# Column attention in an eight-stage transformer kernel: plain query and key projections, their split parts placed by DMA instead of computed in place

## The chip, the cores and the metric

The kernel runs on one core of one Trainium2 chip. The metric is the device time of one execution in microseconds. TensorE (PE) does matmuls, VectorE (DVE), ScalarE (ACT) and GpSimd (POOL) the elementwise work; SyncE (SP) only issues DMA transfers, in the order in which its program lists them.

## The reference, cut to what matters

The model is six residual stages with layer norms. The change touches only the last one, the attention in `_L1_ffn_ref`, which attends along the columns of a 16 x 256 x 128 tensor after a reshape:

```
ln1 = _ln(hidden_states, ln1_weight, ln1_bias)
qkv = (ln1 @ qkv_weight.T).reshape(S, B, N_KV, (Q_PER_KV + 2) * HEAD_DIM)
q = qkv[..., :q_dim]; k, v = ...               # 16 query heads, 8 key/value heads of 8
scores = einsum('sbhd,tbhd->bhst', q, k) / sqrt(8)
attn = softmax(where(causal, scores, -1e9))
```

A head has only 8 dimensions, so a score matmul contracts over very few rows. The scores are wanted to near float32, while the fast matmul type (fp32r) rounds its operands. So the kernel writes q = q_hi + q_lo and k = k_hi + k_lo and contracts over 24 rows that hold the products q_hi k_hi + q_hi k_lo + q_lo k_hi.

## The kernel before, in words

The stage is `column_attention` (line 2379 on). It works on 8 groups of 512 tokens (`U = 8`, index u), and each group has 8 pairs of heads (`PAIRS`), so 64 pair steps g. In pair step g, PE makes the straight scores of pair g (two mask matmuls `bar`, L2569, and 8 score matmuls, L2575), DVE takes their row maxima (L2905), and PE makes the transposed scores of pair g - 11 (L2584, `LAG = 11`), which now include the maxima as two more rows; ACT exponentiates them (L2767). Every second step PE multiplies four heads' probabilities with the values (`values`, L2597).

PE may begin the masks of pair g + 1 only when DVE has finished the maxima of pair g (`negmax_ready`): a chain from PE to DVE to PE runs through every step. Everything else is hung on the steps by the list `stages` (offset, name): a stage with offset o runs for group u in step 8u + o, after the step's scores, and each engine's program is that order, fixed. So step 8u + r repeats for every group, and I call it step r of a group below. `PlannedRing` deals out four PSUM banks by planned hold times; a stage that opens a bank waits until the bank's last reader is done.

Around the change:

- `wq`, `wk` (`cq_pad`, `ck_pad`) are padded weights: for every group of four heads, 4 x 32 columns, in which the 8 columns of a head stand three times. They are copied out of a transposed PSUM tile by nine small activations at the start (L2707, L2709).
- `project` (L2554) is one matmul of 128x128 by 128x512 in float32 for each of the six pieces q0, k0, q1, k1, q2, q3, in steps 5, 6, 7 of the group before and 0, 1, 3 of the own one (offsets -3, -2, -1, 0, 1, 3).
- `round_qk` (ACT, L2731 and L2733) rounds a piece to fp32r; the key's pad rows get ones. `split_qk` (DVE, L2834) computes rounded * split + PSUM, where `split` is 0 or -1 or so by row, and so makes hi or lo rows; it writes straight into `qT` or `kT`, [128, 4 or 2, 512], which the score matmuls read. It also frees the bank.
- `place_rows` (SP, L3001): four transfers of 16 KB put the row maxima into two rows of every head in `qT`.
- `hold_clock` (L232) issues dummy matmuls in steps 0 to 10, while there are no transposed scores yet, and in the drain.

Of the kernel before, what the change touches and what calls it, by code (L numbers as in the profile page):

```python
# [2393 lines left out]
def column_attention(nc, A, K, x_in, R, acc_all, hn_rows):  # L2394
# [6 lines left out]
    with ExitStack() as ctx:  # L2401
# [10 lines left out]
        def sets(n, name, shape, dt=F32):  # L2412
# [8 lines left out]
        split, pad_ones = K["split"], K["pad_ones"]  # L2421

        wq = sb("cq_pad", [P, GROUPS, 4, 32])
        wk = sb("ck_pad", [P, KG, 4, 32])
# [29 lines left out]
        rounded = sets(2, "c_rounded", [P, W], F32R)  # L2454
        qT = sets(2, "cqT", [P, GROUPS, W], F32R)
# [25 lines left out]
        v_cleared = sem("c_values_cleared")  # L2481
        masks_ready = sem("c_masks_ready")
# [7 lines left out]
        rounded_ready = Counted(sem("c_rounded_ready"))  # L2490
        scores_full = Counted(sem("c_scores_full"))
# [29 lines left out]
            (-3, "q0"), (-2, "k0"), (-1, "q1"), (0, "k1"), (1, "q2"), (3, "q3"),  # L2521
# [6 lines left out]
        projections = [("q", 0), ("k", 0), ("q", 1), ("k", 1), ("q", 2), ("q", 3)]  # L2528

        def turn_of(u, name, g):  # L2530
            return len(projections) * u + projections.index((name, g))
# [4 lines left out]
        def _(pe):  # L2536
# [13 lines left out]
            def project(u, name, w, g):  # L2550
                if name == "q" and g == 0:
                    ring.wait_read(pe, "lnT", u)
                ps = ring.open(pe, name, u, g, held=0.95)
                pe.matmul(ps[:], w[:, g].rearrange("p j d -> p (j d)"), lnT[u][:], start=True, stop=True)\  # L2554
                    .then_inc(ring.filled(name, u, g), 1)

            def v_(u):
                if u == 0:
                    pe.wait_ge(w_ready, 1)
# [12 lines left out]
            def scores(n, i, t):  # L2572
                u, p = divmod(n, PAIRS)
                g, j = p // 2, 32 * (2 * (p % 2) + i)
                mm = pe.matmul(s_ps[:, i, t, :], qT[u][j:j + 3 * DH3, g, t * P:(t + 1) * P],  # L2575
                               kT[u][j:j + 3 * DH3, g % KG, t * P:(t + 1) * P], start=False, stop=True, skip_group_check=True)
                if t == TG - 1:
                    mm.then_inc(scores_full.sem, 1)

            def scores_T(n, i, t):  # L2580
                u, p = divmod(n, PAIRS)
                g, j = p // 2, 32 * (2 * (p % 2) + i)
                rows_read = 3 * DH3 + 2
                mm = pe.matmul(t_ps[:, i, t, :], kT[u][j:j + rows_read, g % KG, t * P:(t + 1) * P],  # L2584
                               qT[u][j:j + rows_read, g, t * P:(t + 1) * P], start=False, stop=True, skip_group_check=True)
# [16 lines left out]
            def pair_step(g):  # L2602
# [21 lines left out]
                if turned:  # L2624
                    n = g - LAG
                    if n % PAIRS == 0:
                        pe.wait_ge(*rows_placed.at(64 * (n // PAIRS + 1)))
# [63 lines left out]
            for g in range(KG):  # L2691
                steps[f"k{g}"] = lambda u, g=g: project(u, "k", wk, g)
            for g in range(GROUPS):
                steps[f"q{g}"] = lambda u, g=g: project(u, "q", wq, g)
# [6 lines left out]
        def _(act):  # L2701
            act.wait_ge(cleared, 2)
# [664 lines left out]
```

## Time and profile before

| | us |
|---|---|
| median of 3 runs | 1921.08 (1919.87 to 1923.79) |
| the profiled execution | 1923.63 |
| its span | 1921.9 |
| mean granted TensorE clock, share of full | 0.947 |

Over the whole span PE is busy 89%, DVE 72%, ACT 62% and POOL 54%. The column attention lies from about 1409 to 1659 us of the span. Its first straight scores start at 1425.3 us, those of step 11 at 1452.7, and the last at about 1607; then the last eleven pairs' transposed scores, the output projections and the router drain until 1659. Before and after it stand stages that the change does not touch; each ends with a meeting of all engines. In a row of a timeline the columns are start, duration, engine, line, operation, output and inputs, count, and in brackets the engine's idle time before it and what ended it. A matmul's own duration contains its fill and drain; what it costs its engine is the distance to the next start.

### The profile page before, as it was taken

What the parts mean: (1) busy time and instruction counts of PE and PEld (TensorE: products, weight loads), DVE (VectorE), ACT (ScalarE), POOL (GpSimd) and SP (SyncE); (2) the same over time, 40 slices, a digit from 0 to 9 for tenths busy, and PEclk for the clock granted to TensorE, in tenths of its full rate; (3) what the DMA queues carried; (4) which work ended last, traced back from release to release, by engine and by line L of the source; (5) the groups of instructions that cost most, each with busy time, mean ns of one, the idle gap of its engine ahead of it and who ended that gap; (6) DMA issues with size and microseconds to landing.
All of it is one profiled execution on the core that took longest, in us unless ns stands there. A gap on an engine that the chain in (4) does not pass through costs nothing. (4 is left out here: it accounts for less than half of the span.)

```text
span 1921.9 us, 43928 instructions
## 1 busy us (share of the span) xinstructions
PE 1709.4 (89%) x15676; PEld 1307.0 (68%) x15676; DVE 1376.4 (72%) x4609; ACT 1189.0 (62%) x2858; POOL 1037.9 (54%) x1590
## 2 busy tenths in 40 slices
PE   7999999989889999999999999999879999589930
PEld 4666666656777777777777777776656667479930
DVE  6788888872767788888888888988657876611127
ACT  3566666643688877778878777776315776244412
POOL 3466676663255665656666566666422432175375
PEclk9999999998899999999999999999888999689975
DMA  3000000000300000000000000000000000345322
GB/s 60 6 13 16 16 16 16 12 5 10 92 1 2 1 2 7 8 7 8 7 9 7 8 2 6 5 5 9 6 24 15 27 21 16 99 70 76 59 65 84
DMA packets 57824, 44.03 MB, mean 23 GB/s; under 512 B 13952, under 2 KB 50186, under 8 KB 57482
## 3 DMA queue, kind: packets, MB, share of 16 engines
q1 hardware_dynamic: 52330, 30.11, 5.5%
q0 software_dynamic: 4608, 9.45, 3.4%
q8 instruction: 129, 2.11, 0.5%
q10 hardware_dynamic: 672, 1.67, 0.2%
q14 instruction: 85, 0.70, 0.1%
HBM read 26.52 MB, written 13.63 MB: 21 GB/s over the span
## 5 line engine op out<-in xcount | busy, mean ns | idle before, releaser
L2288 POOL TENSOR_SCALAR probs<-probs,rsums 128x128 f32<-128x128 f32 (+1 forms) x512 | 208.6, 426 | 294.8 <-DVE rsums L2185 293.9
L1061 POOL TENSOR_SCALAR at_least<-magnitudes,candidates 128x512 bf16<-128x512 f32 x128 | 198.2, 1564 | 149.2 <-DVE candidates L950 149.2
L1906 ACT ACTIVATE probs<-probs,low 128x130 f32<-128x130 f32 (+1 forms) x512 | 227.7, 460 | 6.3 <-DVE low L2169 6.2
L2169 DVE CUSTOM_DVE_ANT_0 probs<-dist,pq,nmin 128x128 f32<-128x128 f32 (+1 forms) x512 | 181.2, 409 | 67.6 <-PE pq L1622 67.5
L1021 DVE TENSOR_REDUCE negmax<-ps_scores 128x4 f32<-128x1024 f32 x128 | 156.2, 1221 | 51.3 <-PE ps_scores L629 49.6
L812 ACT ACTIVATE pT<-ps_scoresT 128x1024 f32<-128x1024 f32 x128 | 131.1, 1024 | 63.6 <-PE ps_scoresT L638 57.3
L2179 DVE COPY pT<-pq 128x384 f32<-128x384 f32 x256 | 129.8, 547 | 3.8 <-PE pq L1637 3.8
L1817 ACT ACTIVATE qn<-pq 128x512 f32<-128x512 f32 x128 | 77.2, 603 | 72.2 <-PE pq L1479 70.5
L1622 PE MATMUL pq<-k1T,q1T 64*128 64x128 f32 (+1 forms) x1024 | 119.3, 351 | 0.5 <-ACT k1T L1832 0.4
L3309 POOL DMA_INDIRECT m_x<-token_rows,m_idx_put x80 | 75.7, 947 | 80.2 <-DVE m_idx_put L3239 33.3
L3261 DVE COPY m_y<-pm 128x256 f32<-128x256 f32 x40 | 17.0, 424 | 140.0 <-PE pm L3147 140.0
L1906 ACT ACTIVATION_READ_ACCUMULATOR probs<-probs,low 128x1 f32 x512 | 104.3, 204 | 0.0
L2094 DVE TENSOR_REDUCE ss<-sq 128x8 f32<-128x512 f32 x128 | 84.2, 675 | 26.0 <-ACT sq L1820 25.1
L2905 DVE TENSOR_REDUCE cnegmax<-pc_scores 128x8 f32<-128x1024 f32 x64 | 78.2, 1222 | 25.6 <-PE pc_scores L2575 25.5
L1637 PE MATMUL pq<-ident,probs 128*128 128x128 f32 x512 | 91.3, 274 | 0.0
L2942 POOL TENSOR_SCALAR crstd<-cmv 128x4 f32<-128x4 f32 x16 | 3.7, 233 | 159.6 <-DVE cmv L2816 159.6
L2767 ACT ACTIVATE cpT<-pc_scoresT 128x1024 f32<-128x1024 f32 x64 | 65.5, 1024 | 33.6 <-PE pc_scoresT L2584 33.4
L1622 PEld LDWEIGHTS pq<-k1T,q1T 64*128 64x128 f32 x1024 | 67.5, 187 | 23.2 <-issue 22.2
L1657 PE MATMUL pr_heads<-pT,v 128*64 128x256 f32 x512 | 83.2, 404 | 0.1
L1671 PE MATMUL pr_out<-wo,o1T 128*128 128x128 f32 x512 | 78.5, 276 | 3.5 <-DVE l_r L2026 3.5
L1634 PE MATMUL pq<-ident,probs 128*128 128x128 f32 x256 | 77.3, 302 | 3.7 <-POOL probs L2288 3.6
L3147 PEld LDWEIGHTS pm<-m_w,m_hid 128*128 128x128 f32 x640 | 77.6, 192 | 2.0
(546 smaller groups left out, 5296.1 us busy)
## 6 DMA issues: line engine op xcount, KB each, us to landing
expert_answers<-m_y SPq DMA_DIRECT2D x40, 128.0 KB, 2.1
m_w<-in_L_ffn_moe_w_dram SPq DMA_DIRECT2D x16, 256.0 KB, 5.9
x<-in_x_dram SPq DMA_DIRECT2D x16, 128.0 KB, 2.2
x_mid<-x SPq DMA_DIRECT2D x16, 128.0 KB, 1.8
y<-x_mid SPq DMA_DIRECT2D x16, 128.0 KB, 2.3
x_mid<-y SPq DMA_DIRECT2D x16, 128.0 KB, 1.8
cx<-x_mid SPq DMA_DIRECT2D x8, 256.0 KB, 2.9
token_rows<-c_hn SPq DMA_DIRECT2D x8, 256.0 KB, 2.0
```

Of the source, the lines that this page charges most:

```text
L812: act.activation(pT[:, n % NPT].rearrange("p i k n -> p (i k n)"), t_ps[:].rearrange("p i k n -> p (i k n)"), ACT.Exp).then_inc(pT_ready.s ...
L1021: dve.tensor_reduce(negmax[u][:, :, j:j + 2, q].rearrange("p t j -> p j t"), s_ps[:], AX.X, ALU.max, negate=True).then_inc(negmax_ready.se ...
L1061: pool.tensor_scalar(at_least[:, a, :], mags[:, 512 * (a // 2):512 * (a // 2) + 512], cf[:, a:a + 1], None, ALU.is_ge).then_inc(mask_ready ...
L1622: mm = pe.matmul(ps[i][:, t * P:t * P + w], q1T[u][64 * i:64 * i + 64, p, t * P:(t + 1) * P], k1T[u][64 * i:64 * i + 64, p, 0:w], start=Tr ...
L1637: mm = pe.transpose(ps[:, (kt + 1) * P:(kt + 2) * P], probs[:, a + 1, first_key + kt * P:first_key + (kt + 1) * P], ident[:])
L1657: pe.matmul(tgt[:, 0:N], v1[u][:, 0, h * DH1:(h + 1) * DH1], pT[:, b, 0:2].rearrange("k t q -> k (t q)"), start=True, stop=False, skip_gro ...
L1671: mm = pe.matmul(y_ps[:, u % 2, t * D:(t + 1) * D], o1T[:, n % 4, t * P:(t + 1) * P], wo1[:, p, :], start=(p == 0 and t == 0), stop=False, ...
L1906: ins = act.activation(probs[:, a, keys_nulls(i, w)], probs[:, a, keys_nulls(i, w)], ACT.Exp, bias=low[:, a, i:i + 1], scale=-1.0, accum_o ...
L2094: dve.tensor_reduce(ss[:, a, t, 8 * j:8 * j + 8], sq[:, j, :].rearrange("p (h d) -> p h d", d=DH1), AX.X, ALU.add).then_inc(ss_ready.sem, 1)
L2169: ins = dve.tensor_tensor_reduce(probs[:, a + t, keys(i, w)], dist[:, (1 - t) * P:N], ps[:, t * P:t * P + w], slopes[h], nmin[u][:, t, h:h ...
L2179: dve.tensor_copy(pT[:, (2 * m + i) % 4].rearrange("k t q -> k (t q)"), ps[:, 0:3 * P])\
L2288: ins = pool.tensor_scalar(probs[:, a + t, keys(i, w)], probs[:, a + t, keys(i, w)], rsums[:, a + t, i:i + 1], 1.0, ALU.mult, ALU.mult)
```

## The change

All six padded projections are replaced by two plain ones, q (128 columns, all 16 heads) in step 2 of the group before and k (64 used columns) in step 3 of it. ACT rounds each once, DVE makes the rest (PSUM minus rounded) once, into `q_parts` and `k_parts`. Seven transfers on SP's queue then place the parts into the heads' rows: hi, hi, lo and a row of zeros for q (256 KB of destination each), hi, lo, hi for k (128 KB each). A head now takes 32 rows, in which dimension d has rows 4d to 4d + 3; the key's fourth rows are ones, set once at the start, and the two row maxima go into two of the query's fourth rows. The scores contract over 32 rows instead of 24 and 26. `qT` gets a third buffer. The first scores of group u wait for the seven transfers.

```diff
-        wq = sb("cq_pad", [P, GROUPS, 4, 32])
-        wk = sb("ck_pad", [P, KG, 4, 32])
+        wq = sb("cq_turned", [P, 4, DH3, GROUPS])
+        wk = sb("ck_turned", [P, 2, 4, DH3, KG])
...
-        rounded = sets(2, "c_rounded", [P, W], F32R)
-        qT = sets(2, "cqT", [P, GROUPS, W], F32R)
+        q_parts = sets(2, "cq_parts", [P, 2, W], F32R)
+        k_parts = sets(2, "ck_parts", [64, 2, W], F32R)
+        no_rows = sb("c_no_max_rows", [P, W])
+        qT = sets(3, "cqT", [P, GROUPS, W], F32R)
...
-            (-3, "q0"), (-2, "k0"), (-1, "q1"), (0, "k1"), (1, "q2"), (3, "q3"),
+            (-6, "q"), (-5, "k"),
...
-            (-3, "split_q0"), (-2, "split_k0"), (-1, "split_q1"), (0, "split_k1"), (1, "split_q2"), (3, "split_q3"),
+            (-6, "rest_q"), (-5, "rest_k"), (-5, "place_qk"),
...
-                mm = pe.matmul(s_ps[:, i, t, :], qT[u][j:j + 3 * DH3, g, t * P:(t + 1) * P],
-                               kT[u][j:j + 3 * DH3, g % KG, t * P:(t + 1) * P], start=False, stop=True, skip_group_check=True)
+                mm = pe.matmul(s_ps[:, i, t, :], qT[u][j:j + 32, g, t * P:(t + 1) * P],
+                               kT[u][j:j + 32, g % KG, t * P:(t + 1) * P], start=False, stop=True, skip_group_check=True)
...
-                    if p % 2 == 0:
-                        ring.wait_read(pe, "q", u, p // 2)
-                        if p // 2 < KG:
-                            ring.wait_read(pe, "k", u, p // 2)
+                    if p == 0:
+                        pe.wait_ge(*qk_placed[u % 2].at(PLACED * (u // 2 + 1)))
...
-            for n in range(3):
-                for i in range(2):
-                    act.activation(wq[:, KG * i:KG * i + KG, :, n * DH3:(n + 1) * DH3], w_ps[:, :, :, i * DH3:(i + 1) * DH3],
-                                   ACT.Copy, scale=1 / math.sqrt(DH3))
-                act.activation(wk[:, :, :, n * DH3:(n + 1) * DH3], w_ps[:, :, :, 2 * DH3:3 * DH3], ACT.Copy)
+            for i in range(2):
+                act.activation(wq[:, :, :, KG * i:KG * i + KG].rearrange("k a d g -> k g a d"),
+                               w_ps[:, :, :, i * DH3:(i + 1) * DH3], ACT.Copy, scale=1 / math.sqrt(DH3))
+            act.activation(wk[:, 0].rearrange("k a d g -> k g a d"), w_ps[:, :, :, 2 * DH3:3 * DH3], ACT.Copy)
...
+            def round_qk(u, name, parts, p):
+                ps = ring.wait(act, name, u)
+                if u >= 2 and name == "q":
+                    act.wait_ge(*qk_placed[u % 2].at(PLACED * (u // 2)))
+                act.activation(parts[u][:, 0, :], ps[0:p, :], ACT.Copy).then_inc(rounded_ready.sem, 1)
...
+            def rest_qk(u, name, parts, p):
+                ps = ring.bank(name, u)
+                dve.wait_ge(*rounded_ready.at(2 * u + (1 if name == "q" else 2)))
+                dve.tensor_tensor(parts[u][:, 1, :], ps[0:p, :], parts[u][:, 0, :].bitcast(F32), ALU.subtract)\
+                    .then_inc(ring.read(name, u), 1)
...
+            pool.memset(no_rows[:], 0.0)
+            for i in range(3):
+                ins = pool.memset(kT[i][:].bitcast(F32), 1.0)
+            ins.then_inc(keys_set, 1)
...
-                    for j in range(4):
-                        sy.dma_start(qT[u][32 * j + 3 * DH3:32 * j + 3 * DH3 + 2].bitcast(F32),
-                                     rowsT[u][8 * j:8 * j + 8].bitcast(F32)).then_inc(rows_placed.sem, 16)
+                    sy.dma_start(qT[u][3:P:16].bitcast(F32), rowsT[u][:].bitcast(F32)).then_inc(rows_placed.sem, 16)
+
+                def place_qk(u):
+                    placed = qk_placed[u % 2].sem
+                    if u == 0:
+                        sy.wait_ge(keys_set, 1)
+                    if u >= 3:
+                        sy.wait_ge(*pT_ready.at(PAIRS * (u - 2)))
+                    ring.wait_read(sy, "q", u)
+                    for part, half in enumerate((0, 0, 1)):
+                        sy.dma_start(qT[u][part:P:4].bitcast(F32), q_parts[u][:, half, :].bitcast(F32)).then_inc(placed, 16)
+                    sy.dma_start(qT[u][3:P:4].bitcast(F32), no_rows[:]).then_inc(placed, 16)
+                    ring.wait_read(sy, "k", u)
+                    for part, half in enumerate((0, 1, 0)):
+                        sy.dma_start(kT[u][part:P:4].bitcast(F32), k_parts[u][:, half, :].bitcast(F32)).then_inc(placed, 16)
```

## Rows read from the trace of the kernel before

**Rows 1.** Busy time by engine in stretches: length, PE, PEld, DVE, ACT, POOL, PEclk, DMA.
```profile
1425.30:1452.70 27.40, 24.83 (x188) 15.77 (x188) 21.38 (x30) 7.24 (x12) 9.37 (x16) 0.94 0.02 6
1518.10:1591.30 73.20, 68.12 (x1070) 50.23 (x1068) 58.12 (x118) 51.59 (x73) 25.70 (x33) 1.00 0.07 23
1591.30:1610.10 18.80, 16.56 (x312) 12.58 (x311) 14.56 (x29) 12.23 (x18) 5.64 (x7) 1.00 0.06 21
```

**Rows 2.** Timeline of PE through one steady group, step 1 to step 0.
```profile
1518.12 0.39 PE L2569 MATMUL pc_scores<-c_barred,c_one_hot 24*128 24x512 bf16 x2
...
1519.69 1.13 PE L2554 MATMUL pc<-clnT,cq_pad 128*128 128x512 f32 x2 [0.78 <-DVE ckT L2834]
...
1522.48 0.39 PE L2569 MATMUL pc_scores<-c_barred,c_one_hot 24*128 24x512 bf16 x2
...
1524.61 0.39 PE L2569 MATMUL pc_scores<-c_barred,c_one_hot 24*128 24x512 bf16 x2 [0.70 <-DVE cnegmax L2905]
...
1529.71 0.39 PE L2569 MATMUL pc_scores<-c_barred,c_one_hot 24*128 24x512 bf16 x2
...
1532.94 0.39 PE L2569 MATMUL pc_scores<-c_barred,c_one_hot 24*128 24x512 bf16 x2
...
1536.38 0.39 PE L2569 MATMUL pc_scores<-c_barred,c_one_hot 24*128 24x512 bf16 x2
...
1540.07 0.39 PE L2569 MATMUL pc_scores<-c_barred,c_one_hot 24*128 24x512 bf16 x2
...
1542.52 0.39 PE L2569 MATMUL pc_scores<-c_barred,c_one_hot 24*128 24x512 bf16 x2
```

**Rows 3.** Timeline of PE, last group, where no projections of a next group are left.
```profile
1602.17 0.39 PE L2569 MATMUL pc_scores<-c_barred,c_one_hot 24*128 24x512 bf16 x2 [0.73 <-DVE cnegmax L2905]
...
1604.49 0.39 PE L2569 MATMUL pc_scores<-c_barred,c_one_hot 24*128 24x512 bf16 x2
...
1607.14 0.39 PE L2569 MATMUL pc_scores<-c_barred,c_one_hot 24*128 24x512 bf16 x2
...
1609.96 0.43 PE L2649 MATMUL pc<-c_ident_r,c_rows 128*32 128x128 f32 x4
```

**Rows 4.** Groups of instructions by shape within that steady group: busy, mean ns, idle before.
```profile
L2905 DVE TENSOR_REDUCE cnegmax<-pc_scores 128x8 f32<-128x1024 f32 x8 | 9.8, 1220 | 3.3 <-PE pc_scores L2575 3.3
...
L2584 PE MATMUL pc_scoresT<-cqT,ckT 26*128 26x128 f32 x64 | 6.0, 304 | 0.0
L2575 PE MATMUL pc_scores<-ckT,cqT 24*128 24x128 f32 x64 | 5.9, 301 | 0.0
...
L2834 DVE SCALAR_TENSOR_TENSOR cqT<-c_rounded,split_rows,pc 128x512 fp32r<-128x512 f32 x4 | 3.0, 748 | 0.7 <-ACT c_rounded L2731 0.2
```

**Rows 5.** Timeline of all engines at the start of the stage.
```profile
1409.30 2.73 POOL L2924 MEMSET cv<- 128x1024 f32 x3
...
1416.16 1.11 DVE L2826 TENSOR_SCALAR cxn<-cx,cmv,crstd 128x128 f32<-128x128 f32 x4 [1.53 <-POOLq L2951]
...
1423.05 0.71 DVE L2834 SCALAR_TENSOR_TENSOR cqT<-c_rounded,split_rows,pc 128x512 fp32r<-128x512 f32 x1
...
1425.32 0.39 PE L2569 MATMUL pc_scores<-c_barred,c_one_hot 24*128 24x512 bf16 x2 [1.70 <-issue]
```

**Rows 6.** Timeline of SP's queue in a steady group.
```profile
1518.83 2.59 SPq L3001 DMA_DIRECT2D cqT<-c_rowsT  x4
1521.46 0.39 SPq L2989 DMA_DIRECT2D cx<-x_mid  x1
```

**Rows 7.** DMA issues of the stage (KB, landing), packets and share in 1545.8:1549.5.
```profile
cx<-x_mid SPq DMA_DIRECT2D x8, 256.0 KB, 2.9
...
q1 hardware_dynamic: 164, 0.29, 26.9%
```

**Rows 8.** PE at step 11, and the stretch behind it (columns as in Rows 1).
```profile
1452.69 0.39 PE L2569 MATMUL pc_scores<-c_barred,c_one_hot 24*128 24x512 bf16 x2 [1.35 <-DVE cnegmax L2905]
...
1454.00:1458.00 4.00, 4.00 (x28) 2.30 (x26) 2.42 (x3) 2.18 (x3) 0.00 (x0) 0.50 0.01 4
```

More of the change, by code:

```diff
@@ L2490, in column_attention @@
         rounded_ready = Counted(sem("c_rounded_ready"))
+        qk_placed = [Counted(sem(f"c_qk{i}_placed")) for i in range(2)]
         scores_full = Counted(sem("c_scores_full"))
@@ L2548, in ln_T, with project, v_ @@
                 mm.then_inc(ring.filled("lnT", u), 1)
[L2550 to L2557, printed above, removed]
+            def project(u, name, w):
                 if u == 0:
                     pe.wait_ge(w_ready, 1)
+                ring.wait_read(pe, "lnT", u)
+                ps = ring.open(pe, name, u, held=0.95)
+                pe.matmul(ps[:], w, lnT[u][:], start=True, stop=True).then_inc(ring.filled(name, u), 1)
+            def v_(u):
                 ring.wait_read(pe, "lnT", u)
@@ L2582, in scores_T @@
                 g, j = p // 2, 32 * (2 * (p % 2) + i)
[L2583 to L2585 removed]
+                mm = pe.matmul(t_ps[:, i, t, :], kT[u][j:j + 32, g % KG, t * P:(t + 1) * P],
+                               qT[u][j:j + 32, g, t * P:(t + 1) * P], start=False, stop=True, skip_group_check=True)
                 if t == TG - 1:
@@ L2690, in _ @@
             steps = dict(lnT=ln_T, v=v_, turn_rows=lambda u: u < U - 1 and max_rows(u), back=back, project_out=project_out, hT=h_T, logits=router)
-            for g in range(KG):
-                steps[f"k{g}"] = lambda u, g=g: project(u, "k", wk, g)
+            steps["q"] = lambda u: project(u, "q", wq[:].rearrange("p j d g -> p (j d g)"))
+            steps["k"] = lambda u: project(u, "k", wk[:].rearrange("p a j d g -> p (a j d g)"))
             for g in range(GROUPS):
-                steps[f"q{g}"] = lambda u, g=g: project(u, "q", wq, g)
                 steps[f"heads_T{g}"] = lambda u, g=g: heads_T(GROUPS * u + g)
@@ L2722, in norm1 @@
                 affine(lnT[u][:], ps[:], ln1).then_inc(ring.read("lnT", u), 1)
-            def round_qk(u, name, g):
-                n = turn_of(u, name, g)
-                ps = ring.wait(act, name, u, g)
-                if n >= 2:
-                    before = projections[(n - 2) % len(projections)]
-                    ring.wait_read(act, before[0], (n - 2) // len(projections), before[1])
-                if name == "q":
-                    act.activation(rounded[n][:], ps[:], ACT.Copy).then_inc(rounded_ready.sem, 1)
-                else:
-                    act.activation(rounded[n][:], ps[:], ACT.Identity, bias=pad_ones[:]).then_inc(rounded_ready.sem, 1)
+            def round_qk(u, name, parts, p):
[3 more added lines that the diff above has]
+                act.activation(parts[u][:, 0, :], ps[0:p, :], ACT.Copy).then_inc(rounded_ready.sem, 1)
             def read_v(u):
@@ L2776, in _ @@
             steps = dict(lnT=norm1, v=read_v, turn_rows=lambda u: u < U - 1 and max_rows(u), back=back, hT=h_T, logits=router)
-            for name, g in projections:
-                steps[f"{name}{g}"] = lambda u, name=name, g=g: round_qk(u, name, g)
+            steps["q"] = lambda u: round_qk(u, "q", q_parts, P)
+            steps["k"] = lambda u: round_qk(u, "k", k_parts, 64)
             with act.Fori(0, NG // U) as it:
@@ L2909, in _ @@
                          residual0=lambda u: residual(u, 0), residual1=lambda u: residual(u, 1), pick=pick, masks=masks)
-            for name, g in projections:
-                steps[f"split_{name}{g}"] = lambda u, name=name, g=g: split_qk(u, name, g)
+            steps["rest_q"] = lambda u: rest_qk(u, "q", q_parts, P)
+            steps["rest_k"] = lambda u: rest_qk(u, "k", k_parts, 64)
             for g in range(GROUPS):
@@ L3009, in store_rows @@
                     sy.dma_start(token_rows[u], hn[u][:]).then_inc(hn_stored[u % 2], 16)
-                run_in_order(stages, PAIRS, U, dict(load=load, turn_rows=place_rows, hT=store_rows), pair_step)
+                run_in_order(stages, PAIRS, U, dict(load=load, turn_rows=place_rows, place_qk=place_qk, hT=store_rows), pair_step)
                 for i in range(2):
```

20 lines of the change are left out of this document (5 added, 15 removed).

## The prediction

> **What bounds the kernel now.** I read three views in this order. First the busy time by stretches: in the steady stretch 1518.1 to 1591.3 (three groups of 24.4 us) PE is busy 68.1 of 73.2 us at full granted clock, DVE 58.1, ACT 51.6, and the DMA engines are nearly idle at 0.07 [rows 1]. So PE is the engine that could be the bound, at 93%, and DVE is next at 79%. Then PE's timeline through one group, because a share says nothing of which wait ends last in a step. The starts of the mask matmuls give the step lengths [rows 2]: step 1 takes 4.36 us, step 2 2.13, steps 3 and 4 5.10 together, step 5 3.23, step 6 3.44, step 7 3.69, step 0 2.45; in sum 24.40. Two kinds of step stand side by side. In most PE simply has that much to do. Step 2 ends with PE idle for 0.70 us behind DVE's maxima: this is the chain scores, maxima, next masks, and it gives the least length of a step, 2.13 us. Step 1 holds a third thing, PE idle for 0.78 us before q2, because its bank still waits for DVE's split of k1 [rows 2].
>
> The third view is the same kernel's own experiment. In the last group there is no next group to project for, so its steps 5, 6 and 7 lack q0, k0 and q1. They take 2.32 and 2.65 us, and step 7 2.82 up to the row matmuls that follow it [rows 3], against 3.23, 3.44 and 3.69. So taking a projection off a step is worth 0.91, 0.79 and 0.87 us there. The removed matmuls are on the path.
>
> **Part 1: a steady group.** Step by step, with 0.85 us for a projection (the mean of those three) and 0.75 for a DVE pass over 128x512 [rows 4]:
> - Steps 5, 6, 7 lose a projection each: -2.56 us, read off directly.
> - Step 1 loses q2 and the wait before it. That leaves 4.36 - 0.85 - 0.78 = 2.73; a part of the rest is also behind DVE, and I take -1.7.
> - Step 0 loses k1 but already stands at 2.45, and 2.13 is the least; DVE has the first residual behind the maxima. I take -0.25.
> - Step 3 loses q3 and gains k: 0.
> - Step 2 gains q (0.85), of which 0.70 fills PE's idle time: +0.2. DVE there has maxima 1.22 [rows 4], half a residual with its moments, about 1.3, and the new rest of q 0.75, 3.3 us in one step: it starts the next maxima late. I take +0.25 more in steps 3 and 4.
>
> Sum: -2.56 - 1.7 - 0.25 + 0.45 = -4.06 us a group, 24.4 to 20.3. Bounds: had no step a limit but PE, four projections at 0.91 and the 0.78 would give -4.4; if DVE's 3.3 us step delays everything behind it in full (by 1.2 us, 3.3 less 2.13), -3.1.
>
> The other removed work buys nothing of its own: four ACT roundings and four DVE splits (4 x 0.75 = 3.0 us of DVE's 19.8 a group) lie beside PE. They matter as cover: DVE falls to 17 of 20.3 us, 84%, so it does not take over on average, only in step 2. The score matmuls go from 24 and 26 rows to 32. Rows of 24 cost 301 ns and of 26 304 [rows 4], so I take zero for six to eight more; the bound is that slope of 1.5 ns a row carried on, 128 matmuls x 10 ns, overlapped in pairs: +0.6 us a group, below which nothing speaks for a gain.
>
> **Part 2: how often.** From step 17 to step 57 there are five groups; three are the steady ones (3 x 4.06 = 12.2), and the two before them have not yet all of the back end, so I take 3.9 each: 7.8. In the last group only q2 and q3 go: 2.0 of its 18.8 us [rows 1] (steps 1 and 3, where k has no next group). Steps 11 to 16: a projection each out of five steps, k into one; 3.2. Steps 0 to 10 take 27.4 us, 2.49 each [rows 1]; without projections the chain allows 2.13, with two or three longer ones 24.5 in all, but I take only 2.0 off for the clock (below). Sum: 12.2 + 7.8 + 2.0 + 3.2 + 2.0 = 27.2 us won.
>
> **Part 3: the start.** Here the added path is bare. POOL gets memsets of 3 x 128x1024 and 128x512 before its old three, which took 2.73 us for the same sizes [rows 5]: +3.2 us. POOL stood at the first roots shortly before 1416, so these, and all behind them, come 0.8 us later (DVE already waits 1.53 us for POOL's sequencer there [rows 5]). Now ACT's copies of the weights shrink from nine to three, but ACT was ready before the first norm. PE's q comes in front of v; DVE's rest of q queues behind the mask constants, as the first split does at 1423.05 [rows 5], so rest of q ends about 1424 and rest of k 0.7 later. Then the seven transfers, which the first scores wait for. SP issues one in 0.39 (the load cx) to 0.65 us (each of the four row transfers) [rows 6]: 2.7 to 4.5 us for seven. The data: 704 packets of 2 KB. In the stretch of a load, 164 packets took 26.9% of 16 engines for 3.7 us, 97 ns each [rows 7], so 704 take 4.3 us over 16 engines, mostly beside the issuing. A 256 KB load lands 2.9 us after its issue [rows 7]. From the end of rest of q, T = 3.5 + 2.9 = 6.4 us (4.9 to 8.5). First scores at 1424 + 6.4 = 1430.4 instead of 1425.3: +5.1 (3.6 to 7.2). PE is idle for those microseconds and may begin at a lower clock; of a 2.13 us step 1.22 is DVE's, so 0.9 is PE's, and doubling that once adds 0.9: 6.0.
>
> The Trainium skill, "DMA: Bandwidth & Descriptors", section on the anatomy of one DMA, gives a transfer about 2.0 us plus its bytes at 436 GB/s; by it the 1.44 MB of a group would be an estimated 5.3 us if all were issued at once, so T would be about a microsecond less than mine. No row here shows an SBUF to SBUF transfer of that size, and the sum above does not use it.
>
> **Part 4: the transfers in the steady state.** Rest of q is done about 4 us after the start of step 2, and the scores that need it start with the next group's step 0, 15.5 us after the start of step 2 at the new pace. That leaves 11.4 us for T = 6.4: hidden, with 5 us to spare. SP has nothing else in that time: the load sits in step 2 before it, the rows in step 0 behind it, and the store in step 5 waits only as long as the 4 us of issuing. The wait that `place_qk` adds, for the last exponentials of three groups ago, falls in step 2 and ends before rest of q. The single row transfer is one issue instead of 2.59 us of four, with three steps to land; cost and gain zero. The waits for a bank: with the new order the values of step 1 take the bank of the rows, not that of the heads, so the 0.2 us wait there goes as well.
>
> **The sum.** 27.2 - 6.0 = 21.2 us off the profiled 1923.63, 1902.4. That execution lies 2.55 us above the median of 1921.08, so against the median 1899.9. I predict 1900. The forecast's own range: 3.1 to 4.4 us a group, which scales 27.2 to 21 and 29, less a start of 3.6 to 8, so gains of 13 to 25: 1896 to 1908.
>
> **The rivals.**
> A. The placing takes the place of the projections (slower). In this trace small transfers of one queue run into each other, but no transfer of 256 KB stands directly behind another between SBUF tiles. If they were worked off one after the other at their full landing time, 2.9 for q and about 2.0 for k's halves, T = 4 x 2.9 + 3 x 2.0 = 17.6. Then the first scores come at 1424 + 17.6, a cost of 16.3 + 0.9, and seven groups are late by 17.6 - 11.4 = 6.2 each, 43: net +33, 1954. It decides from where the start, T - 0.4, and the lateness, 7 (T - 11.4), eat up 27.2: T = 13.4 us. Against it: the queue's share is 0.07, and the packets' own time is 4.3 us.
> B. The clock. After PE idled 1.35 us before step 11, the granted clock of the next stretch was 0.50, the lower level of 1.2 GHz, and PE, without a gap, got 28 matmul records done in 4 us [rows 8], where the steady rate (1070 in 73.2 us [rows 1]) is 58. In steps 0 to 10 the projections that go were filling PE; it would now idle 0.8 us in nearly every step. If those eleven steps and the next six run at the lower level, PE's 0.9 us part of the chain grows by half of itself where only straight scores stand and doubles where both do, 0.4 and 0.9 us a step: 10 us of the 21, 1910. The Trainium skill, "TensorE: Matmul & The Clock Gate", section on oscillation, warns of just this: idle gaps between bursts bring the half rate back; the trace agrees at step 11. Against it: the steady step 2 has 0.70 us of idle time at full clock [rows 1, 2], and the dummy matmuls stay.
> C. DVE's step 2 and ACT's exponentials set the pace: only 2.5 us a group, 17 instead of 27 won, 1910.
> D. A and B in part, T near 13: no change, 1921.
>
> **How the numbers follow.** Forecast 0.57, B 0.12, C 0.12, A 0.11, D 0.08. The range takes the forecast, B and C with their bounds: 1892 to 1914. A change of 0.2%, 3.8 us, is about what a measurement of this kernel tells from none. Faster: forecast, B and C, 0.81; same 0.07; slower 0.12 (A and a little of D).
>
> **What would show it.** Group length, from one step 1 to the next: 20.3 us (right), above 21.5 (C), above 26 with PE waiting on a DMA in step 0 (A). Step lengths of 2.3, 2.65 and 2.8 in steps 5, 6, 7, and about 2.7 in step 1. First scores 5 us later after the stage's start, last of the seven transfers landed 6 to 7 us after rest of q. Eleven first steps in about 25 us, granted clock near 1.00 there; near 0.5 shows B. The forecast is wrong if the steady group is not shorter by at least 3 us, or if the first scores come more than 9 us later.

## The result, and the profile after

| | before | after |
|---|---|---|
| median, same chip | 1921.08 us (1915.56 to 1923.79) | 1908.3 us (1902.56 to 1910.37) |
| ratio, 95% interval | | 0.993 [0.9907, 0.9953] |
| profiled execution, span | 1923.63, 1921.9 | 1910.19, 1908.4 |

The changed kernel is faster by 0.7%, 12.8 us of medians. The forecast was 1900 with a range of 1892 to 1914: sign and range hold, the size is 8 us off, and just outside the forecast's own 1896 to 1908. The measured time lies nearer to rival B's 1910 than to the forecast's 1900, and it was for B and C that the range went up to 1914.

The difference of the two profiled executions is 13.4 us, but only a part belongs to the change. The stages ahead of column attention, which the change does not touch, took 1409.0 us before and 1403.2 after. I therefore measure the stage by itself, from its first GpSimd instruction to the first load of the next stage: 250.0 us before, 242.0 after, and 239.2 when the changed kernel was profiled once more (there the stages ahead took 1409.0). So the stage is 8.0 to 10.8 us shorter in the profiled executions, less than the 12.8 of the medians. The profiled executions of the changed kernel are themselves long ones, 1.9 and 8.3 us above the medians of their kernels; a typical one may have a shorter fill than the 50 us read below, which no run here shows. Starts of the mask matmuls, one pair a step, cut the stage into parts (us):

| part | before | after | difference | predicted |
|---|---|---|---|---|
| stage's start to first scores | 16.30 | 21.38 | +5.1 | +5.1 |
| steps 0 to 16 | 43.58 | 50.01 | +6.4 | -4.3 |
| step 16 | 2.77 | 2.64 | -0.1 | |
| steps 17 to 57, five groups | 119.66 | 100.29 | -19.4 | -20.0 |
| steps 57 to 63 | 15.81 | 14.45 | -1.4 | -2.0 |
| step 63 to the end | 51.84 | 53.19 | +1.35 | |

(The 4.3 are the prediction's 2.0 + 3.2 won, less 0.9 for the clock.) Almost the whole miss is in one line: the fill of the pipeline got longer where it should have got shorter. The drain's 1.35 us belongs to that execution; in the second profile of the same kernel it was 51.76. The five groups, too, took less there, 98.73 us: in the first profile the clock was low once more in their first group, whose first step took 3.87 us instead of 2.32. So the groups are worth 19.4 to 20.9 us against 20.0 predicted.

The page of the changed kernel, busy time with its share of the span, and the granted clock in 40 slices:
```profile
span 1908.4 us, 43715 instructions
...
PE 1692.8 (89%) x15612; PEld 1301.9 (68%) x15612; DVE 1353.6 (71%) x4576; ACT 1168.0 (61%) x2820; POOL 1041.1 (55%) x1594
...
PEclk9999999999999999999999999999975999689975
```
Slices 30 and 31 hold the stage's start and fill: digits 7 and 5. That is where most of the missing microseconds are. The next view is busy time in stretches, columns as in [rows 1], the start first, then the fill, the steady state, and the last group:
```profile
1403.20:1424.60 21.40, 10.72 (x37) 6.69 (x38) 10.07 (x43) 3.28 (x10) 10.87 (x19) 0.64 0.38 110
1424.60:1474.60 50.00, 47.20 (x354) 31.81 (x355) 25.85 (x39) 11.28 (x16) 7.98 (x15) 0.54 0.22 67
...
1517.50:1577.50 60.00, 57.39 (x1044) 45.35 (x1044) 49.02 (x108) 43.35 (x61) 25.74 (x34) 1.00 0.32 100
1577.50:1597.00 19.50, 16.61 (x328) 13.67 (x329) 14.17 (x32) 12.24 (x17) 5.64 (x7) 1.00 0.05 18
```
In the steady state PE is busy 57.4 of 60 us at full clock, 96%, DVE 82% and ACT 72%: PE is still the bound, with less slack than before [rows 1]. The fill shows a trap in reading busy shares. PE is "busy" 94% of it, at a granted clock of 0.54, with 354 matmuls in 50 us, where the steady state has 1044 in 60. The same stretch of the kernel before, steps 0 to 16, with more matmuls in less time at 0.84:
```profile
1425.30:1468.90 43.60, 41.03 (x370) 26.13 (x371) 31.25 (x48) 15.70 (x23) 11.22 (x19) 0.84 0.03 9
```

PE's timeline through one steady group after, which answers to [rows 2]:
```profile
1537.56 0.39 PE L2566 MATMUL pc_scores<-c_barred,c_one_hot 24*128 24x512 bf16 x2 [0.45 <-DVE cnegmax L2890]
...
1539.94 0.39 PE L2566 MATMUL pc_scores<-c_barred,c_one_hot 24*128 24x512 bf16 x2
1540.66 1.12 PE L2554 MATMUL pc<-clnT,cq_turned 128*128 128x512 f32 x2
...
1542.16 0.39 PE L2566 MATMUL pc_scores<-c_barred,c_one_hot 24*128 24x512 bf16 x2
1542.90 1.12 PE L2554 MATMUL pc<-clnT,ck_turned 128*128 128x512 f32 x2
...
1545.17 0.39 PE L2566 MATMUL pc_scores<-c_barred,c_one_hot 24*128 24x512 bf16 x2
...
1547.62 0.39 PE L2566 MATMUL pc_scores<-c_barred,c_one_hot 24*128 24x512 bf16 x2 [0.23 <-DVE cnegmax L2890]
...
1549.94 0.39 PE L2566 MATMUL pc_scores<-c_barred,c_one_hot 24*128 24x512 bf16 x2
...
1552.59 0.39 PE L2566 MATMUL pc_scores<-c_barred,c_one_hot 24*128 24x512 bf16 x2
...
1555.42 0.39 PE L2566 MATMUL pc_scores<-c_barred,c_one_hot 24*128 24x512 bf16 x2
...
1557.55 0.39 PE L2566 MATMUL pc_scores<-c_barred,c_one_hot 24*128 24x512 bf16 x2 [0.45 <-DVE cnegmax L2890]
```
The steps are 2.38, 2.22, 3.01, 2.45, 2.32, 2.65, 2.83, 2.13: 19.99 us against 24.40. Steps 5, 6, 7 stand at 2.32, 2.65, 2.83, which are the last group's lengths of [rows 3] to the hundredth. The idle time before q2 is gone, and 0.45 us behind DVE's maxima now end step 0, ahead of step 1's masks.

All engines at the stage's start, which answers to [rows 5]:
```profile
1403.96 2.73 POOL L2910 MEMSET ckT<- 128x1024 f32 x3
...
1411.09 1.12 DVE L2813 TENSOR_SCALAR cxn<-cx,cmv,crstd 128x128 f32<-128x128 f32 x4 [2.31 <-POOLq L2940]
...
1414.40 2.04 PE L2554 MATMUL pc<-clnT,cq_turned 128*128 128x512 f32 x2 [1.02 <-ACT clnT L2708]
...
1417.17 0.69 DVE L2819 TENSOR_TENSOR cq_parts<-pc,cq_parts 128x512 fp32r<-128x512 f32 x1
...
1417.95 1.91 SPq L2999 DMA_DIRECT2D cqT<-cq_parts  x3
...
1419.91 0.61 SPq L3000 DMA_DIRECT2D cqT<-c_no_max_rows  x1
...
1420.56 1.89 SPq L3003 DMA_DIRECT2D ckT<-ck_parts  x3
...
1424.60 0.61 PE L2566 MATMUL pc_scores<-c_barred,c_one_hot 24*128 24x512 bf16 x2 [4.49 <-DMA ckT<-ck_parts]
...
1433.64 1.06 PE L232 MATMUL pc_scoresT<-ident 128*128 128x256 bf16 x4
...
1434.63 0.61 PE L2566 MATMUL pc_scores<-c_barred,c_one_hot 24*128 24x512 bf16 x2
```
SP issues seven transfers in 4.5 us, 0.64 each. From the end of rest of q at 1417.86 to the scores that wait for the last landing it is 6.7 us. PE stands 4.49 us behind that landing, and from there on the half clock is visible in the durations themselves: the pair of mask matmuls takes 0.61 us instead of 0.39 and four dummies 1.06, nine microseconds after the pause.

### The profile page after: what moved, and what is told of

Its sections match the earlier page's. It is cut to its first block and busy times, and to the rows that moved or that the text cites. A ratio compares the mean times of both kernels' runs of the same rounds, so it can differ in the third digit from the quotient of the medians.

```text
span 1908.4 us, 43715 instructions
## 1 busy us (share of the span) xinstructions
PE 1692.8 (89%) x15612; PEld 1301.9 (68%) x15612; DVE 1353.6 (71%) x4576; ACT 1168.0 (61%) x2820; POOL 1041.1 (55%) x1594
```

## The experiments

A second chip was used for the first four kernels; there the kernel before took 1966.39 us. (Its steady groups are 24.40 us there too, by e4, so the difference lies elsewhere.) The later ones ran where it took 1917.53. So times are compared as ratios within one chip (the ratio takes in all runs and need not be the quotient of the medians), and the stage by its own parts, which stand in one profiled execution of each kernel.

The question was what holds the fill at the half clock: PE's pause ahead of step 0, the steps that have little for PE once the projections are gone, or both.

**Fill the pause, fill the steps.** Three kernels change only the number of dummy matmuls that PE runs ahead of a step: 28 instead of 4 ahead of step 0 (e1), 8 instead of 4 ahead of most later ones (e2), both (e3).
```
-  hold_clock(pe, ..., ident, 4)
+  hold_clock(pe, ..., ident, 28 if g == 0 else 4)                                # e1
+  hold_clock(pe, ..., ident, 8 if g and g % 8 not in (2, 3, 4) else 4)           # e2
+  hold_clock(pe, ..., ident, 28 if g == 0 else 4 if g % 8 in (2, 3, 4) else 8)   # e3
```


> The changed kernel with 24 more dummy matmuls on PE in step 0, in front of its wait for the seven transfers (28 instead of 4); nothing else. In the changed kernel PE idles 4.5 us there and the granted clock is 0.50 from step 0 at 1424.6 to about 1471 us: steps 0 to 16 take 50.0 us against 43.6 before. Theory gap (the idle wait for the transfers puts the clock down, and the thin steps then keep it where it is): the steps start at full clock and stay there; steps 0 to 16 in 38 to 40 us, stage 10 us shorter, median near 1898. Rival thin steps (a straight step without projections is too little work for the clock, whatever came before): the first one to three steps are at full clock, then it falls as before; steps 0 to 16 in 47 to 50 us, median 1905 to 1909.

> The changed kernel with 8 instead of 4 dummy matmuls in those of steps 1 to 10 that hold no projection or value matmuls; the idle wait before step 0 is left as it is. Theory gap: the clock is low at step 0 anyway, but rises once PE is busy without a pause, within a few steps; steps 0 to 16 in 42 to 45 us. Rival thin steps: the same, since it is the work in a step that counts: steps 0 to 16 in 41 to 44 us. A rival of both, that the dummies at half clock are simply too long: 8 of them take 2.1 us at the lower level beside a DVE pass of 1.22 us, so steps become 3.4 us instead of 2.7 and steps 0 to 16 take 52 to 54 us if the clock does not come up.

> Both: 28 dummy matmuls in step 0 before the wait for the transfers, and 8 instead of 4 in the steps without projection or value matmuls. Both theories: full clock from step 0 on, steps 0 to 16 in 38 to 40 us, median near 1897, about 10 us below the changed kernel. If this stays slow as well, neither the gap nor the thin steps is the cause.

**The pause alone, in the kernel before.** PE's step 0 also waits for seven GpSimd memsets of 128x1024 into a tile that nobody reads; nothing else changes.
```
+            def gap(u):
+                if u:
+                    return
+                pool.wait_ge(masks_ready, 1)
+                for i in range(7):
+                    ins = pool.memset(idle_tile[:, i], 0.0)
+                ins.then_inc(gap_over, 1)
...
+                        pe.wait_ge(gap_over, 1)     # PE, before step 0
```


> The kernel before, with its own six projections, but PE's step 0 also waits for seven memsets on POOL that start when the masks are ready (7 x 0.91 us): first scores at about 19.7 us after the stage's start instead of 16.3, PE idle for about 5 us before them. No transfers are added. Theory gap: the granted clock then stays low for many steps as in the changed kernel, and steps 0 to 16 take 50 us or more instead of 43.6; median 1930 or above. Rival thin steps: with the projections in place the clock comes back within about two steps, as it did after the 1.7 us pause of the kernel before; only the 3.4 us of later start and up to 2 us of low clock are lost, median 1924 to 1927.

Measured, with the kernel before and the changed one as profiled for the result (us):

| | start to first scores | steps 0 to 16 | steps 17 to 57 | stage | median, ratio |
|---|---|---|---|---|---|
| before | 16.30 | 43.58 | 119.66 | 250.0 | 1 |
| after | 21.38 | 50.01 | 100.29 | 242.0 | 0.993 |
| e1 | 21.41 | 45.72 | 98.75 | 234.8 | 1948.97, 0.9924 [0.9911, 0.9938] |
| e2 | 21.27 | 39.36 | 98.75 | 228.4 | 1942.14, 0.9917 [0.9879, 0.9955] |
| e3 | 21.31 | 39.07 | 98.75 | 228.1 | 1944.39, 0.9917 [0.9892, 0.9942] |
| e4 | 19.56 | 51.00 | 119.66 | 260.4 | 1970.84, 1.0027 [1.0009, 1.0045] |

e1 missed what it was for. PE's timeline there:
```profile
1417.68 3.22 PE L232 MATMUL pc_scoresT<-ident 128*128 128x256 bf16 x28
1425.74 0.60 PE L2566 MATMUL pc_scores<-c_barred,c_one_hot 24*128 24x512 bf16 x2 [4.84 <-DMA ckT<-ck_parts]
```
The 28 dummies ran at full clock, 115 ns each, and were over in 3.22 us; the pause behind them was still 4.84 us, and step 0's mask matmuls are slow again. So e1 and e3 say nothing of a covered pause. But e1 shows the other side: its clock came back after four slow steps, and the fill took 45.72 us, in neither of the expected ranges. Busy time while it was back, and behind that:
```profile
1441.00:1447.00 6.00, 4.38 (x47) 3.32 (x46) 4.74 (x9) 0.38 (x1) 0.00 (x0) 1.00 0.30 66
1448.00:1461.00 13.00, 12.53 (x73) 7.56 (x70) 6.80 (x8) 2.98 (x4) 4.10 (x5) 0.50 0.09 32
```
The clock fell again among thin steps with no idle row above 0.81 us before it; the single executions x3 and x4 below did the same (0.81 and 0.88). e2 is clear: with four more dummies in most steps the fill takes 39.36 us instead of 50.01, less than either theory forecast, although the pause and the first slow steps stand, and the steady state does not pay for them (98.75). e4 shows the other cause. Busy time in four short stretches of it, columns as in [rows 1]: in the pause, in step 0, 10 us after its start, and 17 us after it:
```profile
1421.00:1424.00 3.00, 0.00 (x0) 0.00 (x0) 1.64 (x5) 0.26 (x1) 3.00 (x4) 1.00 0.00 0
1427.00:1430.00 3.00, 3.00 (x10) 1.17 (x10) 1.50 (x2) 0.69 (x1) 3.00 (x5) 0.50 0.00 0
1435.00:1438.00 3.00, 2.19 (x25) 1.49 (x22) 1.61 (x2) 0.00 (x0) 0.00 (x0) 1.00 0.00 0
1442.00:1445.00 3.00, 3.00 (x19) 2.33 (x18) 1.14 (x5) 0.39 (x1) 0.00 (x0) 0.50 0.00 0
```
The kernel before, with all its projections, needs 51.0 us instead of 43.58 for the same 16 steps when PE has stood for 5.49 us first. The pause added 3.3 us by itself and 7.4 in what came behind it. So the loss doesn't need the projections to be gone. The clock did come back in between, and e4 can't say whether its second fall is still the pause's doing. Nor do the whole-kernel times show all of it: the median is 4.45 us above before, where the profiled stage is 10.4 longer.

By the ratios alone e1, e2 and e3 can't be told from the changed kernel: their intervals overlap its [0.9907, 0.9953]. Two of e2's seven runs and two of e3's six lie 9 to 25 us above the others. What they show, they show in the steps of the profiled executions.

**The pause covered, then both.** The changed kernel was run again beside them (a2). In e5 the dummies ahead of step 0 come in five portions, each behind an event that is known to come late enough, so that they can't run out early; e6 also has e3's dummies a step.
```
+  if g == 0:
+      for after, dummies in ((None, 12), ("k", 12), (mv_ready.at(2 * TG), 16),
+                             (xn_ready.at(TG + 1), 8), (xn_ready.at(TG + 2), 4)):
+          ...
+          hold_clock(pe, ..., ident, dummies)
-  hold_clock(pe, ..., ident, 4)                                 # e6 only
+  hold_clock(pe, ..., ident, 4 if g % 8 in (2, 3, 4) else 8)
```


> The changed kernel once more, beside the two that follow: is the low clock of its first 16 steps a matter of one execution? If the cause lies in the kernel (gap or thin steps), steps 0 to 16 again take 46 to 51 us at a mean granted clock near 0.55, and the stage 238 to 242 us. If it was chance, they take about 39 us and the stage is near 229 us.

> The 28 dummy matmuls in one block ran out 4.8 us before the transfers had landed, so the wait was not covered. Here step 0 has 52 dummies (4 a step otherwise, as in the changed kernel), in five portions, each behind an event that comes on its own during the wait (the keys' rest read, the second group's moments, its first two normalized tiles). PE's longest pause before step 0 is then about 1 us. Theory gap: full clock in steps 0 to 3, which were at 0.50 in all kernels so far: 9.5 us instead of 13 to 14. Theory thin steps: those come at full clock too, but then it falls in steps 5 to 10, where a step has only scores and 4 dummies: steps 0 to 16 in 40 to 46 us. If the gap alone is the cause, 36 to 38 us.

> As the kernel before, and 8 instead of 4 dummies in the steps without projection or value matmuls. Both theories: full clock throughout, steps 0 to 16 in 36 to 37 us (16 steps of 2.13 to 2.7), the stage about 226 us long, 16 below the changed kernel; ratio to the kernel before 0.985 to 0.990.

| | start to first scores | steps 0 to 16 | steps 17 to 57 | stage | median, ratio |
|---|---|---|---|---|---|
| a2 | 21.42 | 50.20 | 98.73 | 239.2 | 1905.23, 0.993 [0.991, 0.9951] |
| e5 | 22.37 | 41.70 | 98.72 | 231.7 | 1901.53, 0.991 [0.9893, 0.9928] |
| e6 | 21.34 | 35.18 | 98.73 | 224.6 | 1892.96, 0.9866 [0.9848, 0.9884] |

a2 gives the slow fill again, 50.20 us, step by step within 0.1 us of the first profile nearly everywhere. PE's timeline of e6 ahead of the first scores:
```profile
1419.41 5.45 PE L232 MATMUL pc_scoresT<-ident 128*128 128x256 bf16 x48
...
1425.29 1.48 PE L232 MATMUL pc_scoresT<-ident 128*128 128x256 bf16 x12 [0.43 <-POOL cxn L2950]
...
1427.39 0.39 PE L2566 MATMUL pc_scores<-c_barred,c_one_hot 24*128 24x512 bf16 x2 [0.62 <-DMA ckT<-ck_parts]
```
The pause is down to 0.43 and 0.62 us, and the first mask matmuls take 0.39. Two stretches of each kernel tell the rest. Of a2 the second alone:
```profile
1440.00:1455.00 15.00, 14.24 (x79) 9.41 (x77) 7.75 (x14) 1.29 (x3) 0.10 (x1) 0.50 0.31 97
```
Of e5:
```profile
1425.00:1440.00 15.00, 13.58 (x124) 9.79 (x121) 8.82 (x12) 2.35 (x4) 3.83 (x9) 1.00 0.35 114
1440.00:1455.00 15.00, 13.33 (x84) 8.72 (x84) 7.75 (x12) 1.61 (x3) 4.41 (x6) 0.55 0.13 34
```
Of e6:
```profile
1425.00:1440.00 15.00, 13.39 (x122) 9.81 (x123) 8.49 (x12) 2.35 (x4) 3.69 (x9) 1.00 0.41 129
1440.00:1455.00 15.00, 12.60 (x138) 8.67 (x136) 10.71 (x16) 3.66 (x6) 4.45 (x6) 1.00 0.19 57
```
e5 starts at full clock, does its first seven steps in 2.13 to 2.21 us, then falls to 0.50 all the same, and the seven after them take 2.73 to 3.30 as in a2. e6 keeps 1.00 and every one of those seven at 2.12 to 2.25. So neither cause alone explains it: each loses the clock without the other. Covering the pause is worth 8.5 us with thin steps behind it (a2 to e5) and 4.2 with filled ones (e2 to e6); filling the steps is worth 10.7 with the pause (after to e2) and 6.5 without it (e5 to e6). The two together give 15.0, less than the sum of the larger values, because they pay for the same microseconds. Single executions differ by about 4 us in the fill (see what is left open below), so the 4.2 and the 6.5 are rough; the 15.0 is well clear of that. e6 beats both kernels: its median is 24.6 us below before (25.4 by the stage), twice the change's own 12.3, and its interval, up to 0.9884, lies below a2's, from 0.991. By medians the two remedies together are worth 12.3 us. e5 pays 1.0 us for its dummies at the start, where PE came to them later than in e6, and its median gives back less of the stage's gain than e6's: 16.0 us of 18.3. Its interval overlaps a2's.

**Is PE's time all of it?** The kernel before with its projections q1, q2, q3 and k1 as fp32r matmuls of rounded operands, which take less of PE (a row of 0.50 us where [rows 2] has 1.13), DVE and ACT as they were.
```
+  if (name, g) in (("q", 0), ("k", 0)):
+      weights, tokens = weights.bitcast(F32), tokens.bitcast(F32)
+  pe.matmul(ps[:], weights, tokens, start=True, stop=True)      # tiles now F32R
```


> The kernel before with four of its six projections (q1, q2, q3, k1) as fp32r matmuls in one pass (0.21 us instead of 0.85); their operands are rounded, so the scores lose precision. ACT and DVE keep all six roundings and splits, and there are no transfers. If PE is the bound and the ACT and DVE passes lie beside it, as the prediction says, a steady group loses 4 x 0.64 = 2.6 us by PE and a part of the 0.78 us wait stays: 21.6 to 22.0 us instead of 24.4. Rival: the DVE passes are as much on the path as PE's matmuls, and the group stays above 23.


It came out slower, not faster: stage 262.1 us, 1932.39, groups of 20.02, 23.68, 26.65, 26.91 and 24.9 where before has 24.4. The clock was low for a part of the last three of these. The first two ran at full clock, the 20.02 against 22.04 in the kernel before, the 23.68 against 24.41. PE's timeline in the third, and then the busy time of the second and of a stretch in the third:
```profile
1518.98 0.50 PE L2557 MATMUL pc<-clnT,cq_pad 128*128 128x512 f32 x1 [1.10 <-DVE ckT L2837]
...
1520.75 1.94 PE L2600 MATMUL pc<-cpT,cv 128*32 128x128 f32 x32 [0.84 <-DVEq L2856]
```
```profile
1493.40:1517.10 23.70, 20.38 (x356) 16.15 (x359) 19.79 (x43) 16.83 (x25) 10.04 (x13) 1.00 0.08 27
...
1520.00:1540.00 20.00, 18.95 (x262) 14.99 (x263) 13.67 (x30) 11.72 (x18) 7.37 (x10) 0.74 0.10 31
```
Most of the work taken off PE turned into idle time behind DVE, 1.10 us behind the split of k1 and 0.84 behind another of DVE's instructions, in the full-clock group as here, and then the clock fell. The 21.6 to 22.0 us of the expectation are not met: the one full-clock group that the kernel before does in 24.41 took 23.68, which is the rival's "above 23". With the splits left in place, taking PE's part alone is worth 0.7 us of the 4.4 at full clock, and less than nothing once the clock falls. It is one group of one execution.

**The removed DVE and ACT passes put back.** The changed kernel with four ACT copies and four DVE passes of 128x512 a group, on data that nobody reads.
```
+  act.activation(spare[:, n, :], q_parts[u][:, 0, :].bitcast(F32), ACT.Copy)
...
+  chain(dve.scalar_tensor_tensor(spare[:, 4 + n, :], q_parts[u][:, 0, :].bitcast(F32),
+        iota_one[:, 0:1], q_parts[u][:, 0, :].bitcast(F32), ALU.mult, ALU.add))
```


> The changed kernel with four ACT copies and four DVE passes of 128x512 a group put back where the rounding and splitting of q0, k0, q1, k1 stood (steps 5, 6, 7, 0), on data that nobody reads; PE's work unchanged. The prediction cost the removed passes at nothing beside PE. DVE then has 1.22 + 0.75 us and more a step against steps of 2.13 to 2.82: I expect 20.0 to grow by 0.3 to 1.0 us a group. Rival (they were worth nothing): 20.0 to within 0.1. Rival (they were the real gain): 22 us or more.


The steady group takes 21.80 us instead of 19.99: 1.8, more than the 0.3 to 1.0 expected. Step 6 grew by 0.66 us, step 0 by 0.38 and step 1 by 0.78; the others are what they were. Neighbouring rows of DVE's timeline, then two waits of PE's:
```profile
1541.88 0.72 DVE L2911 SCALAR_TENSOR_TENSOR c_spare<-cq_parts,c_one 128x512 fp32r<-128x512 f32 x1
1542.63 1.23 DVE L2902 TENSOR_REDUCE cnegmax<-pc_scores 128x8 f32<-128x1024 f32 x1
```
```profile
1543.92 0.39 PE L2570 MATMUL pc_scores<-c_barred,c_one_hot 24*128 24x512 bf16 x2 [0.78 <-DVE cnegmax L2902]
...
1555.40 0.66 PE L2655 MATMUL pc<-ident,coT 128*128 128x128 f32 x4 [0.70 <-ACT coT L2765]
```
The busy time of the stretch around them, and a row of the waits (total, times, longest):
```profile
1540.00:1560.00 20.00, 17.41 (x320) 13.76 (x320) 18.11 (x40) 15.10 (x23) 9.14 (x13) 1.00 0.32 104
```
```profile
PEld pc_scores L2570 <- DVE cnegmax L2902: 9.3, 18, 1.0
```
The DVE pass stands directly ahead of a maxima reduction, and the next scores wait for that one: 9.3 us of such waits in the 60 us from 1517.5 to 1577.5, against 6.0 (18 waits too) in the changed kernel. DVE is busy 91% of the stretch. ACT's copies cost as well: in step 6 PE now waits 0.70 us for `coT`, which ACT writes behind such a copy. In this group PE idles 0.77 and 0.78 us behind the maxima where the changed kernel has 0.45, so of the 1.8 about 1.1 are DVE's and 0.7 ACT's. Of the change's 4.4 us a group, 1.8 are thus bound to the passes; that the other 2.6 are the projections' is a difference, not a measurement.

**How far are the transfers from hurting?** Each placing transfer once (x1) and twice more (x2) into spare tiles, awaited by the same scores. SP also waits for the group before's transfers first; that costs nothing, its first issue follows the rest of q within 0.15 us in every group.
```
-  PLACED = 16 * 7
+  PLACED = 16 * 7 * 2      # x2: * 3
+  for more in spare:
+      sy.dma_start(more[part:P:4], q_parts[u][:, half, :].bitcast(F32)).then_inc(placed, 16)
...
```


> The changed kernel with every one of the seven transfers of a group issued a second time into spare tiles, all fourteen awaited before the group's first scores. In the changed kernel the rest of q is read 10.7 us before the scores need it, and the last transfer lands 6.7 us after it (at the start): 4 us to spare. Twice the issuing and bytes add 4.4 us: the first scores come 4.4 us later, and a steady group of 20.0 us grows by 0 to 0.5 us. Rival (transfers of 256 KB are slower than the prediction took them): the first scores come more than 7 us later and a group grows by more than 2 us.

> The same with three of each, twenty-one transfers a group. By the prediction's sum, the time from the rest of q to the last landing is now 6.7 + 2 x 4.4 = 15.5 us against 10.7 that are there: every group is late by about 4.8 us, 24.8 us instead of 20.0, with PE waiting on a DMA in step 0, and first scores 8.8 us later. Rival (the transfers are much cheaper and only the issuing counts, or they hold up something else): less than 22 or more than 27 us a group.


x1: first scores 4.7 us later, groups 20.54 to 22.84 instead of 19.99, more than the 0 to 0.5 expected, stage 248.6, 1915.86. x2: first scores 9.8 us later, groups 27.4 to 29.3 where 24.8 was expected, stage 298.7, 1967.51. A wait of x1 and one of x2 in their PE timelines, and then, of x2, the busy time of stretches ahead of it and behind it:
```profile
1474.48 0.61 PE L2568 MATMUL pc_scores<-c_barred,c_one_hot 24*128 24x512 bf16 x2 [2.70 <-DMA c_spare_k<-ck_parts]
```
```profile
1519.13 0.61 PE L2568 MATMUL pc_scores<-c_barred,c_one_hot 24*128 24x512 bf16 x2 [5.78 <-DMA c_spare_k<-ck_parts]
```
```profile
1505.00:1509.00 4.00, 3.67 (x84) 3.19 (x82) 3.48 (x8) 2.86 (x4) 0.00 (x0) 1.00 1.03 382
1521.00:1525.00 4.00, 4.00 (x47) 3.22 (x49) 3.59 (x9) 2.85 (x4) 0.00 (x0) 0.50 0.18 45
```
At the stage's start seven more transfers land 4.7 us later, and seven more again 5.1. The steady state has 11.4 us for them. Of the seven, the last lands 6.5 to 8.3 us after the rest of q (groups 3 to 7 of both profiles of the changed kernel), 3.1 to 4.6 before the scores. Fourteen take 11.6 to 12.8 in x1 and are late in every group, by up to 2.7 us; 21 take 16.8 to 18.1 in x2. The groups of x2 lose 8.4 to 9.3 us each against the changed kernel: the wait, 5.78 us here, and the half clock that it leaves behind, which the expected 24.8 had left out. Rival A's mechanism exists, then: it begins at twice the traffic and decides at three times.

**The rows.** The changed kernel with scores over 24 of the 32 rows.
```
-  qT[u][j:j + 32, g, ...], kT[u][j:j + 32, g % KG, ...]
+  qT[u][j:j + 24, g, ...], kT[u][j:j + 24, g % KG, ...]
```


> The changed kernel, whose score matmuls contract over 24 of the 32 rows of a head (so the last two dimensions of every head are left out). If rows cost nothing, as the prediction took it, a steady group stays at 20.0 us to within 0.1. Its bound was 0.6 us a group if 1.5 ns a row were real: then 19.4.


The steady group takes 19.97 us against 19.99. Rows between 24 and 32 are free here.

## Why the prediction was right, and where it was wrong

- **Steps 5, 6, 7, read off the last group.** Right to 0.01 us. A kernel's own last iteration, where work is already missing, was the best row of all.
- **The steady group, 20.3.** 19.99. Step 1 went by 1.98, not 1.7, and step 0 by 0.32, not 0.25; steps 2 to 4 grew by 0.45, as predicted, only less of it in step 2 (0.09) and more behind it. The miss is 0.35 a group. Part 2 also counted three steady groups and two lesser ones; of the five from step 17 on four are steady, by their lengths before (22.04, then 24.41 each time). So 20.0 stood against 19.4 and 20.9 measured. The last group gave 1.4, not 2.0.
- **The passes "buy nothing of their own".** Wrong: putting them back costs 1.8 us of the 4.4 (x4), and shortening PE's part alone gave 0.7 (x5). I had called them cover and read DVE's mean share, 79% before, as room. But a pass is paid where it stands ahead of something that PE waits for next: on DVE a maxima reduction, on ACT the copy `coT`. The sum came out because the last group, which also lacks the splits, had both effects in its step lengths; that it did was luck, since the step lengths were priced as PE's work alone.
- **The start, +5.1 and T = 6.4.** First scores +5.08, T 6.7; the rest of q ended 0.3 us earlier than taken, which makes up for it. The 5.3 us that the prediction works out beside its sum from the Trainium skill, "DMA: Bandwidth & Descriptors", section on the anatomy of one DMA, is 1.4 below this: the fit there is for transfers that GpSimd issues, and the estimate has all seven issued at once, while SP takes 4.5 us to issue them.
- **The transfers are hidden.** They are, with 3.1 to 4.6 us to spare and not 5: in the steady groups T is 6.5 to 8.3 us, not 6.4. x1, late in every group, bears out the smaller margin. Rival A falls for seven transfers.
- **Zero for the rows.** 32 rows cost 0.02 us a group more than 24 (x3), and the bound was 0.6.
- **Steps 0 to 16, "without projections the chain allows 2.13", and 0.9 us for the clock.** This is the term that failed: -4.3 predicted, +6.4 measured. The chain does allow 2.13: e6 does the 16 steps in 35.18 us, 8.4 less than before, and its steps 0 to 10 in 24.3, where the prediction had 24.5. But it allows it at full clock. The changed kernel ran them at 0.54. Rival B named the mechanism and the signal, "near 0.5", with 10 us; it came true beside the forecast's steady groups and start. I gave it 0.12. That the measured time still lies in the range is B's doing: by the forecast's own terms it would have ended at 1908. Two things misled me: I took the pause's price as one step at the lower clock, and the steady step 2 with its 0.70 us of idle time at full clock [rows 1, 2] as evidence that idle time of that size does no harm. One such step between full ones is not a row of sixteen. e5 shows such a row falling to 0.50 after seven of them, and e4 that a pause of 5.49 us costs the kernel before 7.4 us behind it.

The Trainium skill, "TensorE: Matmul & The Clock Gate", section on oscillation, says that long idle waits between bursts bring the half rate back, and the section behind it, on a second failure mode, that small but frequent idles of PE can do the same. The traces agree with both: e4 and x2 with the first (5.49 and 5.78 us of idle time, 0.50 behind them), e5 with the second (0.50 behind steps whose longest idle row is 0.81 us).

Left open: how the 2.6 us that x4 leaves over divide between the projections and the wait before q2; what the fill takes in a typical execution; why single executions of e1, x1, x3 and x4 have fills of 45.7 to 47.9 us where after and a2 have 50.0 and 50.2 (the clock comes back a few steps sooner, and nothing in the edits asks for it).

## What to carry to other kernels

Work that is taken off TensorE in a latency-bound stretch, a pipeline's fill above all, can cost more than it gave: check the granted clock there, not the busy share, which reads 94% at half rate. A new wait costs its length and what runs at the lower clock behind it; dummy matmuls cover it only if they are paced by events, because at full clock they run out in half the time. And a pass on an engine at 72 to 82% is not free if it stands ahead of the instruction that PE waits for: ask where it stands, not how full the engine is.

## What the runs showed of the hardware

- The granted clock stayed at its lower level, 1.2 GHz, for most of 50 us of dependent steps (2.1 us each at the full clock), in two executions alike, and fell to it from the full 2.4 GHz with no idle stretch of a microsecond before (e5, and e1, x3, x4 once it had come back).
- Transfers between SBUF tiles of 256 KB, with every fourth partition as their target: SP takes 0.61 to 0.65 us to issue one at the stage's start. A load from memory takes it 0.39 [rows 6], and 0.59 right behind these transfers. Three copies of each, issued one behind the other, fill the 16 DMA engines for 4 us, share 1.03 at 382 GB/s (x2).
- Eight more contraction rows in an fp32r matmul of 128 columns: 304 ns at 32 rows, as at 26, 301 at 24 [rows 4].
